# A three-layer graph network and a mixture of experts on one core: streamed router, gates' parts on ACT and POOL, the next x turned ahead of the down products

## What is computed

```
h = layernorm(x)
for l in 0, 1, 2:                      # graph layers
    agg = segment_sum(h[src], dst) / max(degree, 1)
    h = agg @ Wl[l] + bl[l] + h @ Wr[l]
    h = where(h >= 0, h, a[l] * h)
x = x + h
n = layernorm(x)                       # experts
probs = softmax(n @ Wr + br)           # 8 experts
cw = the two largest probs in their places, else 0
out = sum over e of cw[:, e] * (relu(n @ W1[e] + b1[e]) @ W2[e] + b2[e])
return x + out
```

## Time and profile before

| what | us |
|---|---|
| median of 3 runs | 2534.85 |
| lowest of them | 2533.58 |
| the profiled execution | 2537.42 |
| its span, first to last instruction | 2535.6 |
| busy in the span: PE, PEld, DVE, ACT, POOL | 2492.7, 1624.6, 1874.8, 1491.9, 1106.9 |

### The profile page before, as it was taken

The page is one execution under the profiler, slowest core; times in us unless marked ns, Lnnn a source line. Parts: engine busy times, 40 slices in busy tenths (PEclk is TensorE's granted clock), DMA queues, the critical chain, the costliest instruction groups (busy, mean ns, idle before and its releaser), DMA issues.

```text
span 2535.6 us, 40119 instructions
## 1 busy us (share of the span) xinstructions
PE 2492.7 (98%) x9827; PEld 1624.6 (64%) x9827; DVE 1874.8 (74%) x4816; ACT 1491.9 (59%) x3550; POOL 1106.9 (44%) x1451
## 2 busy tenths in 40 slices
PE   8999999999999999999999999999999999999999
PEld 4444455555488874555558886555546888888887
DVE  5555565555599985555579996557748999999997
ACT  2222245555288875555548886555535666666665
POOL 3222245555144435555433333555534544444452
PEclk9999999999999999999999999999999999999999
DMA  5444468888355547888735555998852334533332
GB/s 149 133 133 133 130 201 265 272 266 271 96 166 165 163 162 254 273 263 273 248 96 166 164 165 188 337 335 271 271 184 80 103 106 137 168 117 93 105 102 70
DMA packets 208171, 460.89 MB, mean 182 GB/s; under 512 B 34896, under 2 KB 35208, under 8 KB 208005
## 3 DMA queue, kind: packets, MB, share of 16 engines
q0 software_dynamic: 64928, 207.55, 29.3%
q1 hardware_dynamic: 73812, 125.17, 14.1%
q10 hardware_dynamic: 69264, 126.12, 13.6%
HBM read 245.32 MB, written 213.93 MB: 181 GB/s over the span
## 4 chain that ended last, share of the span: by engine, by line
PE 79%; DVE 14%; issue 3%; DMA 1%; ACT 1%; POOL 0%; ACTq 0%; SPq 0%; DVEq 0%; POOLq 0%
PE psY L695 11%; PE psM L809 9%; PE psY L809 9%; PE psH L809 9%; PE psY L709 6%; PE psY L717 6%; PE psY L726 6%; PE psT L675 5%; PE psS L821 4%; PE psS L822 4%; DVE xls L1466 1%; DVE res L1554 1%; DVE res L1540 1%; DVE xcs L1469 1%; DVE rows L1530 1%
## 5 line engine op out<-in xcount | busy, mean ns | idle before, releaser
L566 POOL DMA_INDIRECT rows<-y_rows,lists x471 | 491.7, 1044 | 461.8 <-PE psS L822 339.8
L1359 DVE TENSOR_TENSOR lows<-rows,highs 128x512 fp32r<-128x512 f32 x471 | 325.8, 692 | 356.7 <-ACT highs L977 348.3
L977 ACT ACTIVATE outs<-psS 128x512 f32<-128x512 f32 x471 | 279.6, 594 | 272.2 <-PE psS L822 267.2
L977 ACT ACTIVATE highs<-rows 128x512 fp32r<-128x512 f32 x471 | 294.8, 626 | 147.2 <-ACT outs L977 107.1
L821 PE MATMUL psS<-highs,sel 128*128 128x512 f32 x471 | 346.9, 737 | 10.3 <-ACT outs L977 8.0
L573 POOL DMA_INDIRECT rows<-sum_rows,nodeI x158 | 211.2, 1337 | 313.8 <-DVE rows L1367 298.9
L695 PE MATMUL psY<-wy,res 128*128 128x512 f32 x632 | 286.7, 597 | 0.0
L977 ACT ACTIVATE outs<-psY 128x512 f32<-128x512 f32 x237 | 141.7, 599 | 231.2 <-PE psY L695 221.8
L809 PE MATMUL psM<-wz,res 128*128 128x512 f32 x544 | 255.6, 592 | 0.0
L809 PE MATMUL psY<-wz,res 128*128 128x512 f32 x536 | 251.7, 592 | 0.0
L809 PE MATMUL psH<-wz,res 128*128 128x512 f32 x528 | 248.0, 592 | 0.0
(11 more groups left out here) (201 smaller groups left out, 4893.2 us busy)
## 6 DMA issues: line engine op xcount, KB each, us to landing
sum_rows<-outs ACTq DMA_DIRECT2D x471, 256.0 KB, 3.7
y_rows<-outs SPq DMA_DIRECT2D x237, 256.0 KB, 2.0
rows<-in_x POOLq DMA_DIRECT2D x78, 256.0 KB, 3.2
outs<-in_x SPq DMA_DIRECT2D x78, 256.0 KB
out_rows<-res SPq DMA_DIRECT2D x78, 256.0 KB, 2.9
rows<-y_rows,lists POOLq DMA_INDIRECT x471, 4.3
z_rows<-res SPq DMA_DIRECT2D x13, 512.0 KB, 5.6
res<-z_rows SPq DMA_DIRECT2D x13, 512.0 KB, 4.5
```

The costliest lines, as they stand in the source:

```text
L566: pool.indirect_dma_start(out=rows[:, t % RING, :], out_offset=None, in_=y_d, in_offset=bass.IndirectOffsetOnAxis(ap=col(srcT, t), axis=0) ...
L977: act.activation(o, i_, ACT.Copy).then_inc(signal, 1)
L1359: dve.tensor_tensor(lows[:, t % RING, :], rows[:, t % RING, :], highs[:, g, :].bitcast(F32), ALU.subtract)\
```

## The change

- Router: `wg2` (16 columns) becomes the weights, and both parts of x, now side by side in one tile `x_both`, are streamed as 256 columns, in four matmuls, into 16 partitions of `psM`. ACT copies them negated to `logitT` (`take_logits`), PE turns them back in two transposes (`router_turn`) into another part of `psM`, and DVE sums the parts with one reduction and subtracts the bias.
- The gates' high and low parts leave DVE: ACT makes the high ones (`gates_high`), POOL the low ones (`gates_low`).
- PE: `router_turn(k)` and `x_turn(k+1)` come right behind `up_parts(k)`, ahead of `down_parts(k-2)`.
- ACT: `take_logits(k)` behind `squares(k+1)`, `gates_high(k-1)` behind `gated(k-1)`, and `x_top(k+1)` ahead of `widen_down(k-2)`.
- DVE: inside `experts(k)` the network's step comes first, and `up_wide(k)` and one wide step stand between the logits and their least.
- POOL: `scale_shift(k+2)` ahead of `gather_own(k+4)`, `gates_low(k-1)` first.
- Into the experts: `x_turn(0)` goes ahead of the last `z_product`, `x_parts(0)` ahead of the last `take_z`, the `take_z` are mixed with `experts(-2)` and `experts(-1)`, PE waits for one of the two `z_sb` only at k = 2, and the split of the experts' weights starts one block later, behind `split_small`.

```
@@ pool
             for k in range(NT):
+                if k >= 1:
+                    gates_low(k - 1)
                 if k + 2 < NT:
                     negative_mean(k + 2)
                 gates(k)
+                if k + 2 < NT:
+                    scale_shift(k + 2)
                 if k + 4 < NT:
                     gather_own(k + 4, var_in, 1)
-                if k + 2 < NT:
-                    scale_shift(k + 2)
+            gates_low(NT - 1)
@@ tensor
+                pe.wait_ge(logit_set, k)
+                for q in range(C):
+                    mm = pe.matmul(psM[0:2 * X, 0:2 * P], wg2[:, q, :], x_both[:, :, s, q * P:(q + 1) * P],
+                                   start=(q == 0), stop=(q == C - 1))
+                mm.then_inc(router_ps, 1)
+
+            def router_turn(k):
+                s = k % 2
+                pe.wait_ge(logit_set, k + 1)
                 if k > 0:
                     pe.wait_ge(lg_sb[1 - s], (k - 1) // 2 + 1)
-                for q in range(C):
-                    pe.matmul(psM[:, 0:2 * X], xhs[:, s, q * P:(q + 1) * P], wg2[:, q, :], start=(q == 0), stop=False)
-                for q in range(C):
-                    mm = pe.matmul(psM[:, 0:2 * X], xls[:, s, q * P:(q + 1) * P], wg2[:, q, :], start=False,
-                                   stop=(q == C - 1))
-                mm.then_inc(lg_ps[s], 1)
+                for j in range(2):
+                    mm = pe.transpose(psM[:, (2 + j) * P:(3 + j) * P], logitT[:, j * P:(j + 1) * P], ident[:, :])
+                mm.then_inc(lg_ps, 1)
...
             for k in range(NT):
                 router(k)
                 up_parts(k)
+                router_turn(k)
+                if k + 1 < NT:
+                    x_turn(k + 1)
                 if k == 2:
+                    pe.wait_ge(z_sb[0], LAYERS * uses(0))
                     pe.wait_ge(b2_back, 16)
                 if k >= 2:
                     down_parts(k - 2)
-                if k + 1 < NT:
-                    x_turn(k + 1)
                 up_across(k)
@@ scalar
+            def take_logits(k):
+                s, n = k % 2, k // 2
+                act.wait_ge(router_ps, k + 1)
+                act.wait_ge(lg_ps, k)
+                act.activation(logitT[0:2 * X, :], psM[0:2 * X, 0:2 * P], ACT.Copy, scale=-1.0).then_inc(logit_set, 1)
...
                     h_top(k - 2)
                 if k + 1 < NT:
                     squares(k + 1)
+                take_logits(k)
                 if k >= 1:
                     gated(k - 1)
+                    gates_high(k - 1)
                 if k + 1 < NT:
                     norm(k + 1)
                 exps(k)
+                if k + 1 < NT:
+                    x_top(k + 1)
                 if k >= 2:
                     widen_down(k - 2)
-                if k + 1 < NT:
-                    x_top(k + 1)
@@ vector
                 if own:
+                    dve.wait_ge(lg_ps, k + 1)
+                    parts = psM[:, 2 * P:4 * P].rearrange("p (h r) -> p h r", h=2)[:, :, 0:2 * X]
+                    k_lg = step(dve.tensor_reduce(gate(LG), parts.rearrange("p h (g e) -> p e h g", g=2), AX.XY, ALU.add))
+                    up_wide(k)
                     after(k_lg)
-                    dve.tensor_reduce(stat(LOWEST), gate(LG), AX.X, ALU.min).then_inc(lg_sb[s], 1)
-                    up_wide(k)
+                    k_lg = step(dve.tensor_tensor(gate(LG), gate(LG), bgs[:, :], ALU.subtract))
...
-                if k >= 1:
-                    gate_parts(k - 1)
                 experts(k, ahead=(k + 2 < NT))
```

More of the change, by code:

```diff
@@ L144, in build @@
         h_cross = nc.alloc_sbuf_tensor_at("h_cross", [P, D], F32R, offset=wz_at + 8 * D)
-        xhs = nc.alloc_sbuf_tensor_at("xhs", [P, 2, D], F32R, offset=wy_at)
-        xls = nc.alloc_sbuf_tensor_at("xls", [P, 2, D], F32R, offset=wy_at + 8 * D)
+        x_both = nc.alloc_sbuf_tensor_at("x_both", [P, 2, 2, D], F32R, offset=wy_at)
+        logitT = nc.alloc_sbuf_tensor_at("logitT", [P, 2 * P], F32, offset=wz_at + 12 * D)
+        xhs = x_both[:, 0]
+        xls = x_both[:, 1]
         xcs = nc.alloc_sbuf_tensor_at("xcs", [P, 2, D], F32R, offset=hw_at)
@@ L288, in build @@
         pad_set = sem("pad_set")
+        router_ps = sem("router_ps")
+        logit_set = sem("logit_set")
         mean_in = sem("mean_in")
@@ L651, in gates, with gates_low @@
                 pool.tensor_tensor(gate(CW), gate(LG), gate(EX), ALU.add).then_inc(cw_made, 1)
+            def gates_low(k):
+                s = k % 2
+                high, low = (sm[:, s, a:a + 2 * X].rearrange("p (g e) -> p g e", g=2) for a in (HIGH, LOW))
+                pool.wait_ge(cw_high, k + 1)
+                pool.tensor_tensor(low, sm[:, s, CW:CW + X].unsqueeze(1).to_broadcast([P, 2, X]), high,
+                                   ALU.subtract).then_inc(cw_set[s], 1)
             gather_own(0, xn_ready, LAYERS)
@@ L823, in segment_sum, with x_turn @@
                   .then_inc(seg_ps[g], 1)
+            def x_turn(k):
+                s, n = k % 2, k // 2
+                pe.wait_ge(xn_ready[s], LAYERS * uses(s) + n + 1)
+                pe.wait_ge(xd_set[s], (LAYERS - 1) * uses(s) + n)
+                transposes(psT[s], rows[:, 2 + s, :], xT_ps[s])
             pe.wait_ge(const_set, 10)
@@ L869, in _ @@
                     x_transpose(0, 1, l + 1)
[L870 to L878, removed]
+                z_product(*late[-2], l)
+                if l + 1 == LAYERS:
+                    x_turn(0)
+                z_product(*late[-1], l)
             def router(k):
-                s, n = k % 2, k // 2
+                s = k % 2
                 pe.wait_ge(xh_set, (LAYERS - 1) * NT + k + 1)
                 pe.wait_ge(xl_set, (LAYERS - 1) * NT + k + 1)
+                pe.wait_ge(logit_set, k)
[4 more added lines that the diff above has]
+            def router_turn(k):
+                s = k % 2
+                pe.wait_ge(logit_set, k + 1)
                 if k > 0:
                     pe.wait_ge(lg_sb[1 - s], (k - 1) // 2 + 1)
-                for q in range(C):
-                    pe.matmul(psM[:, 0:2 * X], xhs[:, s, q * P:(q + 1) * P], wg2[:, q, :], start=(q == 0), stop=False)
-                for q in range(C):
-                    mm = pe.matmul(psM[:, 0:2 * X], xls[:, s, q * P:(q + 1) * P], wg2[:, q, :], start=False,
-                                   stop=(q == C - 1))
-                mm.then_inc(lg_ps[s], 1)
+                for j in range(2):
+                    mm = pe.transpose(psM[:, (2 + j) * P:(3 + j) * P], logitT[:, j * P:(j + 1) * P], ident[:, :])
+                mm.then_inc(lg_ps, 1)
             def up_parts(k):
@@ L948, in down_across @@
                   .then_inc(o_ps[s], 1)
-            x_turn(0)
-            all_turns(pe, z_sb, LAYERS)
+            pe.wait_ge(z_sb[1], LAYERS * uses(1))
             pe.wait_ge(ex_set, 2 * C + 1)
@@ L1104, in gated, with gates_high @@
                 g_.then_inc(hg_sb[s], 1)
+            def gates_high(k):
+                s, n = k % 2, k // 2
+                act.wait_ge(cw_made, k + 1)
+                if k > 1:
+                    act.wait_ge(cw_ps, k - 1)
+                act.activation(sm[:, s, HIGH:HIGH + 2 * X].rearrange("p (g e) -> p g e", g=2).bitcast(F32R),
+                               sm[:, s, CW:CW + X].unsqueeze(1).to_broadcast([P, 2, X]), ACT.Copy).then_inc(cw_high, 1)
             def norm(k):
                 s, n = k % 2, k // 2
-                act.wait_ge(shift_in[s], n + 1)
+                act.wait_ge(shift_in, k + 1)
                 act.activation(rows[:, 2 + s, :], kept(place(k)), ACT.Identity, scale=st[:, s, RSTD:RSTD + 1],
@@ L1139, in _ @@
                 exps(k)
+                if k + 1 < NT:
+                    x_top(k + 1)
                 if k >= 2:
                     widen_down(k - 2)
-                if k + 1 < NT:
-                    x_top(k + 1)
             h_top(NT - 2)
             gated(NT - 1)
+            gates_high(NT - 1)
             widen_down(NT - 2)
@@ L1479, in h_parts @@
                                          ALU.mult, ALU.add).then_inc(hid_cross, 1)
[L1481 to L1488, removed]
             def up_wide(k):
@@ L1509, in gate @@
                     return sm[:, s, k:k + size]
[L1511 to L1516, removed]
                 if ahead:
@@ L1530, in experts @@
                     step(dve.scalar_tensor_tensor(v, a, 0.0, avec[:, :], ALU.min, ALU.mult))
+                if own:
+                    after(k_lg)
+                    dve.tensor_reduce(stat(LOWEST), gate(LG), AX.X, ALU.min).then_inc(lg_sb[s], 1)
+                if ahead:
                     dve.wait_ge(xe_in[s], 16 * (na + 1))
@@ L1586, in _ @@
                         end_plan(b // 4)
-                    if l + 1 == LAYERS and b in range(NT - 8 - 8 * C, NT - 8, 2):
-                        split_experts((b - (NT - 8 - 8 * C)) // 2)
+                    if l + 1 == LAYERS and b == NT - 8 - 8 * C:
```

(10 more changed lines are left out.)

23 lines of the change are left out of this document (11 added, 12 removed).

## The result

The changed kernel takes 2591.39 us (median of 4 runs, 2590.22 to 2592.88) against 2537.38 for the one before in the same runs: ratio 1.0219, interval 1.0203 to 1.0236. One of the four runs of the kernel before took 3272.83 us; it is in the median of 2537.38 and not in the ratio. The other three lie between 2533.58 and 2539.91, so by the ratio the change costs about 55 us. The forecast was 2613 within 2570 to 2655. The profiled execution took 2590.22, its span is 2588.4.

A forecast was written before the change was run, and what follows sets the result against it. PE, full before, would wait in a loop through ACT's norm: 8.69 us an iteration for 7.64, 76 x 1.05 = +79.8, less 1 and 0.2, together +78.6. Forecast about 2613 us against the median, range 2570 to 2655.

The forecast's parts named there:

- What bounds the kernel: Experts' stage before the change: PE busy all of a 7.64 us iteration, DVE 7.47, ACT and POOL not full.
- The loop: Experts' stage: hidden turn, ACT's queue to the norm, x_turn, down parts, up_across, hidden turn; period 8.69 us, chance 0.79.
- PE's own sum: Rival, experts' stage: norm ready by 4.28, so PE's 7.41 us sets the period; 2516 us, chance 0.10.
- the sum to 8.69: Experts' iteration from the hidden turn: norm's end at 5.33, 0.15 to PE, then 3.21 on PE, making 8.69 us.
- the two ends: Outside the steady experts' iterations: -1 us at the start, -0.2 for the last iteration, which has no turn.
- the router's result: Experts' iteration: take_logits on ACT waits for PE's router and starts at 2.47 us, a new wait of 0.41.
- The stall of PE: Experts' stage: PE idles 1.2 to 1.3 us each iteration before the transposes of x, until ACT's norm ends.
- PE's terms: Experts' iteration: router 0.46 us instead of 0.81, two added transposes 0.18, slow start 0.09 gone; -0.23 taken, PE alone 7.41.
- The old wait of the norm: Experts' iteration: ACT's wait of 1.0 us for POOL's shift disappears, the shift being there at 3.8.
- The way in: Start of the experts: earlier x_turn(0) and x_parts(0) cost PE about 1 us and return the gap; -1, bounds -4 and +3.
- No net change: Rival, experts' stage: PE neither saves nor stalls, or DVE stays the bound; 7.6 us an iteration, 2531 us, chance 0.06.
- The clock: Rival, experts' stage: with PE's gaps the granted clock falls at times to 1.2 GHz; +94 us on top, 2707, chance 0.05.

The follow-up runs named there:

- experiment 7: Kernel before with only the gates' parts moved from DVE to ACT and POOL and the shift ahead of the gather: 2533.86 us, ratio 0.9993.
- experiment 6: Changed kernel with x_turn(k+1) back behind down_parts(k-2) and the gates' parts on DVE again: 2521.34 us, ratio 0.9941.
- experiment 5: Changed kernel with x_turn(k+1) back behind down_parts(k-2) and the old way into the experts: 2522.27 us, ratio 0.9947.
- experiment 1: Changed kernel with only x_turn(k+1) put back behind down_parts(k-2): 2521.69 us, ratio 0.9945.
- experiment 4: Changed kernel with norm(k+1) on ACT ahead of gated(k-1) and gates_high(k-1): 2523.43 us, ratio 0.995.
- experiment 2: Kernel before with only x_turn(k+1) moved ahead of down_parts(k-2): 2593.5 us, ratio 1.0225.
- Experiment 10: Changed kernel with POOL's old order, the gather ahead of the shift: 2593.67 us, ratio 1.0225.
- experiment 3: Changed kernel with gates_high(k-1) on ACT behind norm(k+1) instead of ahead of it: 2583.93 us, ratio 1.0189.

## Why the prediction was right, point by point

**What bounds the kernel, shown.** PE was full and DVE nearly so: experiment 7 takes 0.3 us off DVE and moves nothing, experiment 6 gives PE less work and gains all there is.

**The loop, shown.** Its place (PE in front of the turn of x), what ends it (ACT's norm) and its reach (all of the stage) are in the rows. Three experiments take one stretch out of it: the period is 8.31 without gates_high, 7.48 without the down products and 7.50 with the norm ahead of gated, the last two being PE's own sum, or within 0.05 of it. With only ACT's old queue ahead of the norm it is 7.73, and it stays at 8.42 where POOL's part is later but not the latest.

**The size, too large.** The step that was mis-sized is the sum to 8.69; the period is 8.41 to 8.42, so 76 x 0.77 = 58 and not 80. In spans the forecast was +78.6 and the traces have +52.8: 21.7 of the difference are the loop, 4.1 the two ends (-5.3 for -1.2), of which 2.6 are the chance named above. By terms: the router's result reached ACT at 2.37 and not 2.47 (the 256-column group is busy 0.63, where I had 0.66, and the hand-over took 0.03 for 0.10); gates_high takes 0.11 of ACT's queue and not 0.20; the norm 0.80 for 0.82; the hand-over to PE is 0.05 for 0.15. From the turn to the hidden turn it was 3.24 for 3.21. ACT's copy of the logits was the other way, 0.28 for 0.27. The terms that missed by much had been taken too high, a hand-over most, since I had taken one that was 0.10 and doubted it upwards; together the errors make 0.27 us, or a third of the measured effect of 0.77. The stall of PE follows: 1.00 an iteration by starts (2201.08 less 2199.90 and two transposes of 0.09), shown as 0.79 of idle in the bracket, where I had 1.2. So ACT's wait in front of the logits' copy is 0.23 and not 0.4, and DVE's two new waits come to 0.96 an iteration, where I had over 1.

**PE's terms, nearly right.** Four 256-column matmuls take 0.46 (2197.61 to 2198.07), as interpolated by width; their slow neighbour is gone (up takes 0.92 behind them, not 1.01). The 0.46 is the stream alone, so the loads of 16 columns are hidden. Whether loads of 128 columns would not have hidden here as well, no run tells. (The rule of the Trainium skill, page "TensorE: Matmul & The Clock Gate", section "LDWEIGHTS (loading the stationary operand)", that a load costs by its columns, is borne out in its direction and not in its size: the profile shows a load of the router with 94 ns at 16 columns and with 190 to 192 ns at 128 columns in the kernel before, where the rule has 13 and 107.) PE's sum is 7.46 to 7.48 rather than 7.41.

**POOL.** The old wait of the norm is gone as said, and the shift is ready earlier (3.36) than I put it (3.8): its last operation took 0.19 us in place of 0.55.

**The way in.** I had -1 with -4 and +3. Tried by itself (experiment 5) it makes no difference beyond the intervals. In the traces of before and after it is -5.3, outside my bounds: 2.6 of chance ahead of it, 1.9 of new order, and 0.9 (all rounded) between the first router and the third, where both are at a lowered clock (0.66 before, 0.79 after).

**The rivals.** PE's own sum as the period was refuted for this kernel, and is what experiments 1 and 4 restore. No net change was refuted by the period, and experiment 7 shows that DVE was not the bound. The clock held: 1.00 in the steady stretches, in spite of the stall in each iteration.

## What to carry to other kernels

When an instruction that waits is moved ahead of work that does not, the moved-over work joins whatever loop the wait closes: sum that loop over all engines, with each in-order queue's neighbours in it, before asking which engine is full. The place in the queue is the price: the same move cost 6, 57 or 70 us here or nothing that could be told, and the move of one 0.11 us instruction 7.5. The longest wait in a list (62 us here) can cost nothing; the one to look for is that of the full engine.

## What the runs showed of the hardware that I had not expected

POOL's last step to the shift (128x1, one multiplication) is shown with 0.19 us in the changed kernel and in the short iterations of experiment 2, and with 0.66 in its long ones, where the chain starts right behind the gather:

```profile
2207.27 0.67 POOL L634 TENSOR_TENSOR st<-st 128x1 f32<-128x1 f32 x1
```

The same instruction with the same operands, so up to 0.5 us for what stands ahead of it. Experiment 10 shows that it is the gather: it differs from the changed kernel in nothing but the gather's place ahead of the chain, and the median of the step is 0.65 there and 0.19 here. In the short iterations of experiment 2, where the chain starts 0.34 us behind the gather instead of at once, the step is back at 0.19. How the gather does it is open.

The granted clock of one short stretch, from the second router to the third, differed between traces of kernels that do the same work there and ahead of it: in experiments 1 and 3 PE had been busy 4.68 of 7.20 us, and the stretch then ran at 0.80 in 8.34 us and at 1.00 in 6.81. A gain of some 2 us ahead of it can vanish so in a trace, and one trace of each kernel does not show it.
